# A linear attention's key and value biases: from a rank-2 term added to each batch's key-value matrix, to a correction computed from the queries

## What is computed

```python
q = (decoder_seq @ Wq.T + bq).reshape(B, T_dec, 16, 32)
k = (encoder_seq @ Wk.T + bk).reshape(B, T_enc, 16, 32)
v = (encoder_seq @ Wv.T + bv).reshape(B, T_enc, 16, 32)
kv = jnp.einsum('bthd,bthe->bhde', k, v)
att = jnp.einsum('bqhd,bhde->bqhe', q, kv) * scale
att = att.reshape(B, T_dec, 512)
return layer_norm(att + decoder_seq, ln_gamma, ln_beta)
```

## Time and profile before

| what | value |
|---|---|
| median of 3 runs | 603.89 us (599.87 to 604.61) |
| the profiled execution, its time | 603.76 us |
| its span in the trace | 602.0 us |
| PE busy | 584.0 us, 97% of the span |
| DVE, POOL, ACT busy | 354.4, 216.9, 198.5 us |
| mean granted clock of PE | 0.991 |

### The profile page before, as it was taken

One profiled execution on the slowest core, in us unless ns is written; L12 is line 12 of the kernel. 1 busy time (PEld: TensorE's weight loads), 2 busy tenths in 40 slices (PEclk: granted clock), 3 DMA queues, 4 the chain that ended last, 5 costly groups with the idle time before them and its releaser, 6 DMA issues.

```text
span 602.0 us, 11557 instructions
## 1 busy us (share of the span) xinstructions
PE 584.0 (97%) x4928; PEld 500.5 (83%) x4928; DVE 354.4 (59%) x399; ACT 198.5 (33%) x254; POOL 216.9 (36%) x183
## 2 busy tenths in 40 slices
PE   5989999999999999999999999899999999999997
PEld 5979888898989889896888977877888788888886
DVE  5799471725546370734686248565656966975641
ACT  3444343505134342503523333313321112433320
POOL 2567764565636264560342000203334254000000
PEclk9999999999999999999989799999999999999999
DMA  8770524242213224014003202106623035398601
GB/s 313 266 278 17 204 72 148 71 148 70 81 68 135 83 70 148 1 47 159 2 2 124 98 3 70 71 1 168 191 71 113 27 140 140 105 228 207 160 0 71
DMA packets 25141, 65.77 MB, mean 109 GB/s; under 512 B 2408, under 2 KB 2408, under 8 KB 22160
## 3 DMA queue, kind: packets, MB, share of 16 engines
q1 hardware_dynamic: 25104, 65.23, 34.5%
HBM read 64.05 MB, written 1.18 MB: 108 GB/s over the span
## 4 chain that ended last, share of the span: by engine, by line
PE 92%; DVE 5%; ACT 1%; issue 1%; DMA 1%; POOL 1%; DVEq 0%
PE ps L317 17%; PE ps L319 17%; PE ps L318 17%; PE ps L831 4%; PE ps L834 4%; PE ps L818 3%; PE ps L822 3%; PE ps L824 2%; PE ps L820 2%; PE ps L819 2%; PE ps L823 2%; PE ps L826 2%; PE ps L833 2%; PE ps L886 2%; PE ps L848 1%; PE ps L1082 1%
## 5 line engine op out<-in xcount | busy, mean ns | idle before, releaser
L458 POOL TENSOR_TENSOR psum_tmp<-psum_tmp,raw 128x512 f32<-128x512 f32 (+1 forms) x88 | 132.0, 1500 | 34.3 <-DVE lo L1331 25.8
L317 PE MATMUL ps<-hi,gh 128*128 128x512 f32 x192 | 76.2, 397 | 0.0
L318 PE MATMUL ps<-lo,gh 128*128 128x512 f32 x192 | 74.8, 390 | 0.0
L319 PE MATMUL ps<-hi,gl 128*128 128x512 f32 x192 | 74.8, 390 | 0.0
L1331 DVE TENSOR_TENSOR lo<-raw,hi 128x2048 fp32r<-128x2048 f32 (+1 forms) x29 | 61.5, 2152 | 21.2 <-ACT hi L531 21.2
L512 POOL TENSOR_TENSOR sx<-sx,raw 128x512 f32<-128x512 f32 x32 | 41.1, 1292 | 89.8 <-DVE raw L1652 89.8
L712 ACT ACTIVATE hi<-raw 128x2048 fp32r<-128x2048 f32 x14 | 26.8, 1913 | 101.6 <-PE ps L319 101.6
L317 PE MATMUL ps<-wvh,gh 128*128 128x512 f32 x128 | 51.3, 400 | 0.0
L319 PE MATMUL ps<-wvh,gl 128*128 128x512 f32 x128 | 50.3, 393 | 0.0
L318 PE MATMUL ps<-wvl,gh 128*128 128x512 f32 x128 | 50.2, 392 | 0.0
L1658 DVE TENSOR_TENSOR lo<-raw,hi 128x2048 fp32r<-128x2048 f32 x15 | 35.3, 2351 | 20.0 <-ACT hi L712 20.0
(11 more groups left out here) (226 smaller groups left out, 1375.8 us busy)
## 6 DMA issues: line engine op xcount, KB each, us to landing
raw<-in_ctx SPq DMA_DIRECT2D x23, 1024.0 KB, 4.9
raw<-in_ve SPq DMA_DIRECT2D x8, 1024.0 KB, 5.4
raw<-in_oe SPq DMA_DIRECT2D x8, 1024.0 KB, 5.6
wk<-gm_rows SPq DMA_DIRECT2D x8, 512.0 KB, 9.0
g<-gm_rows SPq DMA_DIRECT2D x8, 512.0 KB, 9.4
raw<-in_ctx SPq DMA_DIRECT2D x8, 130.0 KB
raw<-in_ctx SPq DMA_DIRECT2D x2, 512.0 KB, 4.6
xres<-in_x SPq DMA_DIRECT2D x1, 1024.0 KB, 10.0
```

The costliest lines, as they stand in the source:

```text
L317: pe.matmul(dst, wh, xh, start=first, stop=False)
L318: pe.matmul(dst, wh, xl, start=False, stop=False)
L319: return pe.matmul(dst, wl, xh, start=False, stop=last)
L458: pool.tensor_tensor(psum_tmp[0:k, :], (raw[:, 0, :] if t == 1 else psum_tmp[0:k, :]), raw[0:k, t, :], ALU.add).then_inc(ctx_sum, 1)
```

## The change

The kv matrices stay without a bias term. Instead the term is applied to the queries. `turn_left` transposes `left` on PE into bank 1 (four transposes), and DVE copies it to `leftT` (128 x 4 x 64). `query_shares` multiplies `leftT` with all queries, one matmul of 128 x 64 weights by 512 columns for each 128 of the width, into banks 2, 1, 0, 2. DVE masks each bank with `batch_of` into `shares` (64 x 512 each), so that a token keeps the rows of its own batch alone. `corrections(i)` multiplies the shares of token tile i with `right`, four matmuls of 64 x 128 by 128 columns, into the attention's bank, and `attend(i)` accumulates its products on top. ACT's eight copies, PE's seven `rank2` and the extra 16 matmuls of `kv_part(7)`, and DVE's seven adds are gone. `w_low(W_Q1, 0)` moves behind the copy of `leftT`, `gl_lower(7)` behind the second mask; the three corrections now stand together ahead of the three attends.

```diff
--- before.py
+++ after.py
@@ -161,8 +161,8 @@
         m_mm, m_done, kv_mm, kv_done = (sem(s) for s in ("m_mm", "m_done", "kv_mm", "kv_done"))
         half_ones, s_mm, srow_done, sT_mm, s_done, r_mm, pick_done = (
             sem(s) for s in ("half_ones", "s_mm", "srow_done", "sT_mm", "s_done", "r_mm", "pick_done"))
-        bk_near, rk_near, rv_sum, right_near, rb_done, r2_mm, r2_done = (
-            sem(s) for s in ("bk_near", "rk_near", "rv_sum", "right_near", "rb_done", "r2_mm", "r2_done"))
+        bk_near, rk_near, rv_sum, right_near, lt_mm, lt_done, uw_mm, uw_done = (
+            sem(s) for s in ("bk_near", "rk_near", "rv_sum", "right_near", "lt_mm", "lt_done", "uw_mm", "uw_done"))
         att_mm, y_done, xb_done, z_done, x1_done, ob_done = (
             sem(s) for s in ("att_mm", "y_done", "xb_done", "z_done", "x1_done", "ob_done"))
         qq_done, vv_mm, vv_done, samepos_done = (sem(s) for s in ("qq_done", "vv_mm", "vv_done", "samepos_done"))
@@ -259,13 +259,12 @@
 
         near_heads = headmask[:, :].rearrange("p (j d) -> p j d", d=D1).unsqueeze(1).broadcast_to([P, KC, 4, D1])
 
-        def right_of(b):
-
-            return raw[0:64, 4 + b, :] if b < B - 1 else psum_tmp[0:64, :]
-
-        def rank2_bank(b):
-
-            return bank[(1, 2, 0, 4, 1, 2, 4)[b]]
+        leftT = psum_tmp[:, 0:KC * 64].rearrange("p (c r) -> p c r", r=64)
+        shares = sx[0:64, 4:8, :]
+
+        def share_bank(c):
+
+            return bank[(2, 1, 0, 2)[c]]
 
         def by_tile(t):
 
@@ -623,16 +622,8 @@
             w_high(W_Q1, 0, 1)
             m_copy(B - 2, (2,))
 
-            def right_part(b):
-                act.wait_ge(right_near, 1)
-                act.activation(right_of(b), right, ACT.Copy, scale=batch_of[:, b:b + 1]).then_inc(rb_done, 1)
-
-            for b in range(4):
-                right_part(b)
             m_copy(B - 2, (3,))
             gh_high(B - 1)
-            for b in range(4, B):
-                right_part(b)
             m_copy(B - 1)
 
             def xT_pair_high(n, h):
@@ -876,21 +867,12 @@
             def kv_part(b):
 
                 pe.wait_ge(m_done, b * 4 + 4)
-                last = isinstance(b, int) and b == B - 1
-                if last:
-                    pe.wait_ge(rb_done, B)
                 for c in range(KC):
                     for k in range(KC):
                         for j in range(4):
                             cols = slice(c * P + D1 * j, c * P + D1 * j + D1)
                             mm = pe.matmul(head_block(bank[6], c, j), wk[:, k, cols], mb[:, k, cols],
-                                           start=(k == 0 and not (last and c)), stop=(k == KC - 1 and not last), skip_group_check=last)
-                if last:
-                    for c in range(KC):
-                        for j in range(4):
-                            cols = slice(c * P + D1 * j, c * P + D1 * j + D1)
-                            mm = pe.matmul(head_block(bank[6], c, j), left[:, cols], right_of(b)[:, cols],
-                                           start=False, stop=True, skip_group_check=True)
+                                           start=(k == 0), stop=(k == KC - 1))
                 mm.then_inc(kv_mm, 1)
 
             def products_of(b, first, halfway, between):
@@ -947,39 +929,49 @@
                     mm = pe.matmul(bank[0][0:32, :], scol[:, k, :], wv_again[:, k, :], start=(k == 0), stop=(k == KC - 1))
                 mm.then_inc(r_mm, 1)
 
-            def rank2(b):
-                if b == 0:
-                    pe.wait_ge(bk_near, 1)
-                    pe.wait_ge(rk_near, 1)
-                pe.wait_ge(rb_done, b + 1)
-                if b == 2:
-                    pe.wait_ge(right_near, 1)
-                if b == 3:
-                    pe.wait_ge(gl_done, 3 * B - 2)
-                if b >= 4:
-                    pe.wait_ge(r2_done, (1, 2, 4)[b - 4])
+            def turn_left():
+
+                pe.wait_ge(bk_near, 1)
+                pe.wait_ge(rk_near, 1)
                 for c in range(KC):
-                    cols = slice(c * P, (c + 1) * P)
-                    mm = pe.matmul(rank2_bank(b)[:, cols], left[:, cols], right_of(b)[:, cols], start=True, stop=True)
-                mm.then_inc(r2_mm, 1)
-
-            def attend(i):
+                    mm = pe.transpose(bank[1][:, c * 64:(c + 1) * 64], left[:, c * P:(c + 1) * P], ident[0:64, 0:64])
+                mm.then_inc(lt_mm, 1)
+
+            def query_shares():
+
+                pe.wait_ge(lt_done, 1)
+                for c in range(KC):
+                    if c == 2:
+                        pe.wait_ge(right_near, 1)
+                    if c == 3:
+                        pe.wait_ge(uw_done, 1)
+                    pe.matmul(share_bank(c)[0:64, :], leftT[:, c, :], qT[:, c, :], start=True, stop=True).then_inc(uw_mm, 1)
+
+            def corrections(i):
 
                 if i == 0:
                     pe.wait_ge(mir_mm, B)
                     pe.wait_ge(g_add, 5 * B)
-                if i == 1:
-                    pe.wait_ge(rk_near, 1)
+                    pe.wait_ge(uw_done, KC)
                     pe.wait_ge(right_near, 1)
-                pe.wait_ge(r2_done, min(2 * i + 2, B - 1))
+                if i == 2:
+                    pe.wait_ge(gl_done, 3 * B - 2)
                 if i == NT - 1:
                     pe.wait_ge(kv_done, B)
                 for c in range(KC):
+                    cols = slice(c * P, (c + 1) * P)
+                    pe.matmul(att_bank(i)[:, cols], shares[:, c, i * P:(i + 1) * P], right[:, cols], start=(c == 0), stop=False,
+                              skip_group_check=True)
+
+            def attend(i):
+
+                pe.wait_ge(kv_done, 2 * i + 2)
+                for c in range(KC):
+                    cols = slice(c * P, (c + 1) * P)
                     for b in (2 * i, 2 * i + 1):
-                        cols = slice(c * P, (c + 1) * P)
                         p0 = S * (b % 2)
                         mm = pe.matmul(att_bank(i)[p0:p0 + S, cols], qT[:, c, b * S:(b + 1) * S], kv[:, b, cols],
-                                       start=True, stop=True)
+                                       start=False, stop=True, skip_group_check=True)
                 mm.then_inc(att_mm, 1)
 
             row_sums()
@@ -990,16 +982,16 @@
             m_part(B - 2, 1, False)
             sum_rows()
             m_part(B - 2, 2, False)
+            turn_left()
             m_part(B - 2, 3, False)
             g_transposes(B - 1)
+            query_shares()
             kv_part(B - 2)
-            for b in range(4):
-                rank2(b)
-            attend(0)
-            attend(1)
-            for b in range(4, B - 1):
-                rank2(b)
-            attend(2)
+            for i in range(NT - 1):
+                corrections(i)
+            for i in range(NT - 1):
+                attend(i)
+
             def transposes_1(i):
 
                 pe.wait_ge(s_norm[2], i + 1)
@@ -1024,12 +1016,12 @@
 
             for m in range(KC):
                 m_part(B - 1, m, False)
-            pe.wait_ge(r2_done, B - 1)
             transposes_1(0)
             transposes_1(1)
             kv_part(B - 1)
             pe.wait_ge(xT_lo, 2 * KC)
             transposes_1(2)
+            corrections(NT - 1)
             attend(NT - 1)
             pe.wait_ge(w_lo, 3)
             project_1(0)
@@ -1456,23 +1448,27 @@
             dve.wait_ge(ld_bk, 16)
             top, low = slice(0, 32), slice(32, 64)
             dve.tensor_tensor(by_tile(left[top, :]), by_tile(left[top, :]), near4(top), ALU.mult).then_inc(bk_near, 1)
-            w_low(W_Q1, 0)
             dve.wait_ge(r_mm, 1)
+            dve.tensor_tensor(by_tile(left[low, :]), by_tile(bank[0][low, :]), near4(low), ALU.mult).then_inc(rk_near, 1)
             dve.wait_ge(ld_bv, 16)
             dve.scalar_tensor_tensor(out=right[top, :], in0=right[top, :], scalar=float(T), in1=bank[0][top, :],
                                      op0=ALU.mult, op1=ALU.add).then_inc(rv_sum, 1)
-            dve.tensor_tensor(by_tile(left[low, :]), by_tile(bank[0][low, :]), near4(low), ALU.mult).then_inc(rk_near, 1)
             dve.wait_ge(rv_sum, 1)
             dve.wait_ge(pick_done, 3)
             dve.tensor_tensor(by_tile(right), by_tile(right), near4(slice(0, 64)), ALU.mult).then_inc(right_near, 1)
-            gl_lower(B - 1)
+            dve.wait_ge(lt_mm, 1)
+            dve.wait_ge(sum_out, B)
+            dve.tensor_copy(leftT, bank[1][:, 0:KC * 64].rearrange("p (c r) -> p c r", r=64)).then_inc(lt_done, 1)
+            w_low(W_Q1, 0)
+            dve.wait_ge(s_mm, 1)
+            for c in range(KC):
+                dve.wait_ge(uw_mm, c + 1)
+                dve.tensor_tensor(shares[:, c, :].rearrange("p (b t) -> p b t", t=S), share_bank(c)[0:64, :].rearrange("p (b t) -> p b t", t=S),
+                                  batch_of[:, :].unsqueeze(2).broadcast_to([64, B, S]), ALU.mult).then_inc(uw_done, 1)
```

(15 more changed lines are left out.)

## The result

| | kernel before | changed kernel |
|---|---|---|
| median | 603.45 us (20 runs, 599.87 to 605.20) | 607.85 us (20 runs, 603.29 to 612.13) |
| profiled execution | 603.76 us, span 602.0 | 610.11 us, span 608.0 |
| its mean granted clock | 0.991 | 0.983 |

The ratio is 1.0076, 95% interval 1.0058 to 1.0094: slower by 0.8%, 4.4 us. I had forecast 605.0 with a range up to 607.0. The sign is the forecast one; the size lies outside the range, by 0.85 us, and most of it arose where I had not looked. Ratios here are not exactly quotients of the medians.

A forecast was written before the change was run, and what follows sets the result against it. PE bounds the kernel, busy 97%; its 2.7 us gain shrinks to 0.3 behind DVE's chain, giving 603.76 - 0.3 = 603.5, plus 1.5 for a clock fall: 605.0 us, range 601.2 to 607.0.

The forecast's parts named there:

- the wait and the low clock: PE's 1.03 us wait before `attend(2)` and the 1.2 GHz clock behind it (losses 0.84 and 0.90 us) would go.
- the gain on PE is eaten by DVE's chain: DVE's layer norm chain starts later, at 298.9, so 2.7 us won on PE become 0.3 us at `attend(3)`.
- The waits of 0.45 and 1.38 us: PE would wait 0.5 us ahead of `transposes_1(1)` and 1.5 us for the low halves ahead of `transposes_1(2)`.
- B: Likeliest rival, chance 0.45: clock falls once before or in `attend(3)`, costing 1.5 us; 605.0 us.
- The forecast's sum up to `transposes_1(3)`: 0.3 us won by `attend(3)`, then 1.5 us lost to the clock's fall there: +1.2 us.
- From there on nothing changes: Behind `attend(3)`, the rest of the kernel keeps its time; profiled time 603.76 - 0.3 = 603.5 us.
- D: Rival, chance 0.04: clock falls at `query_shares` and stays down through the attends, 289.8 to 300.65; about 611 us.
- other places' clock: Clock changes at places other than the changed stretch; chance 0.03, no time given.
- the prediction's own sum: 603.76 us less 0.3 won gives 603.5; plus 1.5 for a clock fall gives 605.0.
- A: Rival, chance 0.27: clock stays up around `attend(3)` and DVE's chain decides; 603.5 us.

The follow-up runs named there:

- e6: Changed kernel with each `attend(i)` right behind its `corrections(i)` for tiles 0 to 2; 606.40 us, ratio 1.0046.
- e2: Changed kernel with 24 one-column matmuls (96 instructions) of padding at the start of PE's list; 603.65 us, ratio 0.9992.
- e11: Changed kernel with 32 one-column matmuls (128 instructions, half a block) of padding at the start of PE's list; 602.71 us, ratio 0.9987.
- e9: Changed kernel with both orders mended (`attend(i)` behind `corrections(i)`, `corrections(3)` ahead of the low halves' wait), no padding; 604.04 us, ratio 1.0022.
- e12: e8 unaltered, run again beside e9, e10 and e11; 601.27 us, ratio 0.9958 to the kernel before.
- e1: Changed kernel unaltered, run and profiled again; 606.43 us, ratio 1.0046 to the kernel before.
- e3: Kernel before with 40 one-column matmuls (160 instructions) of padding at the start of PE's list; 605.46 us, ratio 1.0047.
- e10: Kernel before with 8 one-column matmuls (32 instructions) of padding at the start of PE's list; 603.26 us, ratio 0.9995.
- e8: Changed kernel with the edits of e4 and e6 and 32 one-column matmuls (128 instructions) at the start of PE's list; 600.66 us, ratio 0.9953.
- e4: Changed kernel with `corrections(3)` moved ahead of the wait for the low halves, its `kv` wait removed; 606.55 us, ratio 1.0046.
- e5: Changed kernel with 24 one-column matmuls (96 instructions) put into PE's wait ahead of `transposes_1(2)`; 606.44 us, ratio 1.0054.

## Why the prediction was wrong

Right, step by step:
- `query_shares`: 293.61 - 290.03 = 3.58 us, forecast 3.42. `turn_left` 0.39 us, forecast 0.45. Corrections 0.118 us an instruction (2.84 for 24), forecast 0.120.
- `m_part(7)` at 300.61, forecast 300.75, without the wait and the low clock.
- `part1_out(0)` at 299.06, forecast 298.9; `norm_back(2, 2)` ends at 314.60, forecast 314.45. So the gain on PE is eaten by DVE's chain, as told, and e6 shows it from the other side: with `attend(0)` early the wait is 0.37 us.
- The waits of 0.45 and 1.38 us, forecast 0.5 and 1.5; `attend(3)` at 317.77, forecast 317.65; the clock falls there (B). The forecast's sum up to `transposes_1(3)`, +1.2 us, measured +0.9. The two waits came as told; that the clock fell at them in the profiled execution was a guess with a chance of 0.45 that came true by luck: in the profiles of e2 and e11, whose work there is the same, it did not.

Wrong is the step "From there on nothing changes". It took the untouched code behind the stretch as unchanged in time. The count that it needed can be taken from the first part of the prediction: 88 matmul instructions removed and 44 added, so PE's list gets shorter. I counted instructions by their time alone and not by the place that they give to all later ones. With H1 the missing term has two parts. One is the wait itself, 1.3 to 1.6 us at equal clock (e9 against e12 on one chip; the one execution of e1, 603.7, against e11's 602.1 on another, at 0.997). The other is the clock behind it, in some 3 of 10 executions a stretch of more than 12 us at 0.50 in a stage of small matmuls. Such executions are 5 to 7 us longer than the same kernel's at 0.997 (e3, e1, e9), other falls of the clock included.

Wrong too is rival B's price as an average. The low clock that I found behind the wait at 300 and moved to 317 is not in every execution: the profiles of e3 and e10, the kernel before with padding, have none near 300, those of e2 and e11 none near 317. The kernel before has executions from 599.7 to 608.6 us, at mean clocks from 1.0 down to 0.985. I took one profiled execution as the level, and 607.0 as the end of the range left no room for a second fall. Among the rivals a long low clock stood only at the stretch itself (D), and there it did not happen. The case that came true was among the chances as "other places' clock", at 0.03, with no time and no sign to know it by; the 12 us at 0.50 are of that kind.

With both terms all but taken out by e11 (a wait of 0.30 us is left), the change is worth nothing: 0.9987 (0.9969 to 1.0005). That is the verdict of the prediction's own sum (A or B, within 1.3 us of no change). Against e10, whose later code stands where e11's stands, it is 1.3 us slower at 0.997 and 0.6 at 0.994, while its median is 0.6 lower; how often each falls to a lower clock decides between them, and that stays open.

What stays open as well: why e3 was slowed by 2 us where the changed kernel was by 4.4, although both have the wait. e3 has a second code wait and 3 of 12 low executions, the changed kernel 9 of 20 and e1 only 2 of 12. Six to twenty executions don't fix such a share.

## What to carry to other kernels

Removing or adding instructions moves all later code of that engine against the blocks in which it is read. Before a change is judged, look in the waits for a wait ended by "issue" in the middle of a run of equal matmuls, and time the change once more with half a block (128 instructions) of padding where the engine idles anyway: the part of the result that moves with it is the place of the code and not the work. Time more than one place, for each has its own waits: e2 took the wait out of the near values and got one of 1.33 us at 86 us. And where PE is made faster under cover of another engine's chain, start that chain early (each attend right behind its corrections) rather than batch the new work ahead of it.

## What the runs showed of the hardware

- A wait for code shows in PE's timeline as a gap with the releaser "issue": 0.8 to 1.6 us in the near values at the same instruction in seven kernels, whatever the time at which the stage began (347.0 to 349.3 us), 0.3 us at the 91st in e8 and e11, 2.1 us behind 128 + 29 small matmuls in e3, 1.33 us at 86 us in e2.
- A 16 KB packet on the instruction queue starts 2.3 to 2.9 us ahead of the end of the near values' wait in those seven, and two of them start 3.6 us apart in the changed kernel (348.4 and 352.0), while 128 small matmul instructions with their weight loads, one block, run in 1.63 us.
- A wait for data can hide a wait for code: e4 and e5 filled such a wait, and 0.84 and 1.54 us of code wait appeared.
- Behind the wait in the near values the clock was at 0.50 from 352 to 364 in the changed kernel's profile, and at 1.00 in those of e3, e4, e6 and e9, with waits of 0.87 to 1.07 us at the same instruction. With the code in that place the fall is more frequent, not certain.
